# A feed-forward block whose weights are streamed in 128-column tiles and split beside the products

## The reference

```python
def _lora_linear(x, w, a, b):
    base = jnp.einsum('bsd,od->bso', x, w)
    low = jnp.einsum('bsr,or->bso', jnp.einsum('bsd,rd->bsr', x, a), b)
    return base + low * SCALING          # SCALING = 2, rank 16
h1 = _lora_linear(x, w1, lora_A1, lora_B1)     # 512 -> 1376
h3 = _lora_linear(x, w3, lora_A3, lora_B3)     # 512 -> 1376
g = jax.nn.silu(h1) * h3
return _lora_linear(g, w2, lora_A2, lora_B2)   # 1376 -> 512
```

## Time and profile before

| | us |
|---|---|
| median of 3 runs | 2617.37 (2616.24 to 2623.03) |
| the profiled execution: its time | 2618.33 |
| its span, first to last instruction | 2616.4 |
| TensorE busy (matmul) | 2486.5 (95%) |
| VectorE busy | 1558.7 (60%) |
| ScalarE busy | 1355.7 (52%) |
| GpSimd busy | 1059.2 (40%) |
| mean granted TensorE clock | 0.975 of full speed |

### The profile page before, as it was taken

The page is one execution under the profiler, slowest core; times in us unless marked ns, Lnnn a source line. Parts: engine busy times, 40 slices in busy tenths (PEclk is TensorE's granted clock), DMA queues, the critical chain, the costliest instruction groups (busy, mean ns, idle before and its releaser), DMA issues. The chain is left out here.

```text
span 2616.4 us, 40097 instructions
## 1 busy us (share of the span) xinstructions
PE 2486.5 (95%) x12487; PEld 1839.7 (70%) x12487; DVE 1558.7 (60%) x2791; ACT 1355.7 (52%) x2088; POOL 1059.2 (40%) x1097
## 2 busy tenths in 40 slices
PE   6999999999999999999998599989999999999996
PEld 3677776777777777777774366667887878778774
DVE  5666666666666666666663611066657557557566
ACT  3577777777777777777774300033324324334231
POOL 0455565555556555555653100034234234343220
PEclk8999999999999999999998699989999999999998
DMA  5222222222222222221221500021010010010001
GB/s 190 48 47 55 43 54 49 46 51 51 51 43 54 47 48 51 45 57 43 54 44 57 160 6 0 0 81 41 0 40 16 24 40 16 24 40 16 1 1 53
DMA packets 46694, 116.86 MB, mean 45 GB/s; under 512 B 5313, under 2 KB 22721, under 8 KB 40514
## 3 DMA queue, kind: packets, MB, share of 16 engines
q1 hardware_dynamic: 46658, 116.40, 17.0%
HBM read 71.81 MB, written 10.49 MB: 31 GB/s over the span
## 5 line engine op out<-in xcount | busy, mean ns | idle before, releaser
L472 DVE TENSOR_REDUCE row_max<-ps_max 128x1 f32<-128x512 f32 x1024 | 671.0, 688 | 198.5 <-PE ps_max L539 176.6
L390 POOL TENSOR_TENSOR p_lo<-probs,p_hi 128x1024 f16<-128x1024 f32 x256 | 547.8, 2150 | 387.4 <-ACT p_hi L422 387.1
L417 ACT ACTIVATE probs<-ps_score 128x1024 f32<-128x1024 f32 x512 | 523.2, 1022 | 253.3 <-PE ps_score L554 229.1
L552 PE MATMUL ps_score<-Q,K 128*128 128x512 f32 x1024 | 407.5, 398 | 1.6 <-ACT probs L417 1.5
L554 PE MATMUL ps_score<-Q,K 97*128 97x512 f32 x1024 | 407.0, 397 | 0.0
L539 PE MATMUL ps_max<-KX,Q 68*128 68x512 f32 x1024 | 378.6, 410 | 16.1 <-DMA KX<-content_k 10.3
L466 DVE TENSOR_TENSOR Q<-ps_x,Q 64x512 fp32r<-64x512 f32 x256 | 176.5, 689 | 247.2 <-ACT Q L412 243.5
L422 ACT ACTIVATE p_hi<-probs 128x1024 f16<-128x1024 f32 x256 | 269.5, 1053 | 4.1
L539 PEld LDWEIGHTS ps_max<-KX,Q 68*128 68x128 f32 x1024 | 188.7, 189 | 91.7 <-issue 40.2
L552 PEld LDWEIGHTS ps_score<-Q,K 128*128 128x128 f32 x1024 | 194.4, 190 | 60.9 <-ACT probs L417 13.4
L554 PEld LDWEIGHTS ps_score<-Q,K 97*128 97x128 f32 x1024 | 195.2, 191 | 38.8
(11 more groups left out here) (231 smaller groups left out, 4223.7 us busy)
## 6 DMA issues: line engine op xcount, KB each, us to landing
Q<-Q SPq DMA_DIRECT2D x64, 512.0 KB, 4.3
w_raw<-in_w_qrope SPq DMA_DIRECT2D x32, 512.0 KB, 3.7
wq_raw<-in_wq SPq DMA_DIRECT2D x8, 1024.0 KB, 5.5
wo_raw<-in_wo SPq DMA_DIRECT2D x8, 1024.0 KB, 4.9
w_raw<-in_w SPq DMA_DIRECT2D x6, 704.0 KB, 4.2
Q<-content_q SPq DMA_DIRECT2D x64, 64.0 KB
K<-content_k SPq DMA_DIRECT2D x64, 64.0 KB
wkv_raw<-in_wkv SPq DMA_DIRECT2D x8, 512.0 KB, 3.5
```

Of the source, the lines that this page charges most:

```text
L390: pool.tensor_tensor(p_lo[:, j, :, :], probs[:, j, 0:PAIRED, :], p_hi[:, j, :, :], ALU.subtract)\
L417: act.activation(probs[:, j, 2 * half:2 * half + 2, :], ps_score[half][:, :, :], ACT.Exp, scale=SCALE).then_inc(exped, 1)
L472: dve.tensor_reduce(row_max[:, t, j:j + 1], ps_max[t % 2][:, :], axis=AXX, op=ALU.max)\
L552: pe.matmul(ps_score[half][:, k, :], K1[:, b, t * P:(t + 1) * P], Q1[:, b, j, :], start=True, stop=False)
```

## The change

The feed-forward block is rewritten, with the stage ahead of it.

- The weights w1, w3 and w2 are laid out in memory as 11 tiles of 128 hidden columns, each 128 x 1536 (1024 of w1 and w3, 512 of w2, 768 KB). The loop has 22 steps, one for each half and tile, written out; each step loads its tile (so each tile is loaded twice) into a ring of three.
- The up projections aren't folded any more. Instead u = A x is made once for each half by 12 matmuls (`low_rank`, L1050), scaled by 2, and each projection gets one more matmul, B u (L1069).
- The down weights are still folded, tile by tile: one matmul (`delta_out`, L1042), one addition by VectorE (`fold`).
- w1 and w3 tiles are rounded by ScalarE (L889) and subtracted by GpSimd two steps ahead. w2 and g are split too: 12 rounded matmuls (L1081) stand where four float32 ones stood.
- The factors and the first three tiles are loaded in `merge_heads_stage`, behind wo and x; the factors are split there by ScalarE (after tile 4) and VectorE (after tiles 4, 5 and 6), and the first two weight tiles as well.

The diff, cut to its core:

```diff
+            swiglu_first_loads(sp, dram, ffn)
+        @block.gpsimd
+        def _(pool):
+            for s in range(AHEAD):
+                swiglu_w_low(pool, ffn, s)
+            pool.wait_ge(ffn["w_low"], AHEAD)
...
+                if t == ST:
+                    swiglu_lora_high(act, ffn)
+                if ST < t <= ST + AHEAD:
+                    swiglu_w_high(act, ffn, t - ST - 1)
+            act.wait_ge(ffn["w_high"], AHEAD)
...
+                for part in {ST: (0, 1), ST + 1: (2,), ST + 2: (3, 4)}.get(t, ()):
+                    swiglu_lora_low(dve, ffn, part)
...
+def swiglu_load(sp, dram, m, s):
+    sp.dma_start(m["raw"][:, s % RAW, :], dram["w_ffn"][STEPS[s][1], :, :]).then_inc(m["raw_in"][s % RAW], 16)
...
+def swiglu_lora_high(act, m):
+    act.wait_ge(m["lora_in"], 64)
+    act.activation(m["a_hi"][:, :, :], m["a_raw"][:, :, :], ACT.Copy).then_inc(m["lora_high"], 1)
+    act.activation(m["b2"][:, :], m["b2_raw"][:, :], ACT.Copy).then_inc(m["lora_high"], 1)
+    act.activation(m["a2"][:, :], m["a2_raw"][:, :], ACT.Copy).then_inc(m["lora_high"], 1)
+    for i in range(2):
+        act.activation(m["b"][:, i, :], m["b_raw"][:, i, :], ACT.Copy).then_inc(m["lora_high"], 1)
...
+def swiglu_lora_low(dve, m, part):
+    rows = [slice(32 * k, 32 * (k + 1)) for k in range(3)]
+    dve.wait_ge(m["lora_high"], part + 1)
+    if part == 0:
+        out, raw, high = (m[name][:, :, :] for name in ("a_lo", "a_raw", "a_hi"))
+    elif part == 1:
+        out, raw, high = m["b2"][rows[1], :], m["b2_raw"][rows[1], :], m["b2"][rows[1], :]
+    elif part == 2:
+        out, raw, high = m["a2"][rows[2], :], m["a2_raw"][rows[2], :], m["a2"][rows[2], :]
+    else:
+        i = part - 3
+        out, raw, high = m["b"][rows[1], i, :], m["b_raw"][rows[1], i, :], m["b"][rows[1], i, :]
+    dve.tensor_tensor(out, raw, high, ALU.subtract).then_inc(m["lora_low"], 1)
...
+def swiglu_w_high(act, m, s):
+    act.wait_ge(m["raw_in"][s % RAW], 16 * (s // RAW + 1))
+    act.activation(m["w_hi"][:, s % RING, :, :, :].rearrange("p i c n -> p (i c n)"), m["raw"][:, s % RAW, 0:W13],
+                   ACT.Copy).then_inc(m["w_high"], 1)
+def swiglu_w_low(pool, m, s):
+    pool.wait_ge(m["w_high"], s + 1)
+    pool.tensor_tensor(m["w_lo"][:, s % RING, :, :, :].rearrange("p i c n -> p (i c n)"), m["raw"][:, s % RAW, 0:W13],
+                       m["w_hi"][:, s % RING, :, :, :].rearrange("p i c n -> p (i c n)"), ALU.subtract)\
+        .then_inc(m["w_low"], 1)
+AHEAD = 2
...
+        ps_down, ps_h, ps_delta, ps_u = banks[0:4], banks[4:6], banks[6], banks[7]
...
+            for s in range(RAW, NS):
+                sp.wait_ge(w_low, s - RAW + 1)
+                sp.wait_ge(w2_low, s - RAW + 1)
+                swiglu_load(sp, dram, mem, s)
...
+            def second(s):
+                pool.wait_ge(w2_high, s + 1)
+                pool.tensor_tensor(w2_lo[:, s % RING, :], raw[:, s % RAW, W13:W13 + D], w2_hi[:, s % RING, :],
+                                   ALU.subtract).then_inc(w2_low, 1)
+            for s in range(NS):
+                second(s)
+                if s + AHEAD < NS:
+                    swiglu_w_low(pool, mem, s + AHEAD)
...
+            for s, (half, m) in enumerate(STEPS):
+                if m == 0:
+                    act.wait_ge(u_made, half + 1)
+                    act.activation(u[:, :], ps_u[0:SLOTS, :], ACT.Copy, scale=LORA_SCALE).then_inc(u_high, 1)
+                act.wait_ge(folded, s + 1)
+                if s >= RING:
+                    act.wait_ge(down, s - RING + 1)
+                act.activation(w2_hi[:, s % RING, :], raw[:, s % RAW, W13:W13 + D], ACT.Copy).then_inc(w2_high, 1)
+                if s + AHEAD < NS:
+                    if s + AHEAD >= RING:
+                        act.wait_ge(hidden[1], s + AHEAD - RING + 1)
+                    swiglu_w_high(act, mem, s + AHEAD)
+                act.wait_ge(hidden[0], s + 1)
+                if s:
+                    act.wait_ge(g_made, s)
+                act.activation(gate[:, :], ps_h[0][:, :], ACT.Silu).then_inc(gated, 1)
+                act.wait_ge(g_made, s + 1)
+                if s >= 2:
+                    act.wait_ge(down, s - 1)
+                act.activation(g_hi[:, s % 2, :], g[:, s % 2, :], ACT.Copy).then_inc(g_high, 1)
...
+            def fold(s):
+                dve.wait_ge(delta, s + 1)
                 dve.wait_ge(raw_in[s % RAW], 16 * (s // RAW + 1))
+                dve.scalar_tensor_tensor(out=raw[:, s % RAW, W13:W13 + D], in0=ps_delta[:, :], scalar=LORA_SCALE,
+                                         in1=raw[:, s % RAW, W13:W13 + D], op0=ALU.mult, op1=ALU.add).then_inc(folded, 1)
+            def low_u(half):
+                dve.wait_ge(u_high, half + 1)
+                dve.scalar_tensor_tensor(out=u[64:SLOTS, :], in0=ps_u[64:SLOTS, :], scalar=LORA_SCALE,
+                                         in1=u[64:SLOTS, :], op0=ALU.mult, op1=ALU.subtract).then_inc(u_low, 1)
+            def add_out(half):
+                dve.wait_ge(down, HT * (half + 1))
+                    row = X[:, half * ST + t, :]
+                    dve.tensor_tensor(row, ps_down[t][:, :], row, ALU.add).then_inc(taken, 1)
+            def count_out(half):
+                    dve.wait_ge(taken, half * ST + t + 1)
+                    dve.bn_stats(sb["stats"][:, half * ST + t, :], X[:, half * ST + t, :]).then_inc(counted, 1)
+            for s, (half, m) in enumerate(STEPS):
+                if s == 0:
+                    fold(0)
+                if m == 0:
+                    low_u(half)
+                if s + 1 < NS:
+                    fold(s + 1)
+                if half and m == 1:
+                    add_out(0)
+                dve.wait_ge(gated, s + 1)
+                dve.wait_ge(hidden[1], s + 1)
+                if s >= 2:
+                    dve.wait_ge(g_low, s - 1)
+                dve.tensor_tensor(g[:, s % 2, :], ps_h[1][:, :], gate[:, :], ALU.mult).then_inc(g_made, 1)
+                dve.wait_ge(g_high, s + 1)
+                dve.tensor_tensor(g_lo[:, s % 2, :], g[:, s % 2, :], g_hi[:, s % 2, :], ALU.subtract).then_inc(g_low, 1)
+                if half and m == 1:
+                    count_out(0)
+            add_out(1)
+            count_out(1)
...
+            TERMS = ((0, 0), (1, 0), (0, 1))
+            x = (xh, xl)
+            def delta_out(s):
+                m = STEPS[s][1]
+                if s:
+                    pe.wait_ge(folded, s)
+                pe.matmul(ps_delta[:, :], mem["a2"][:, m * P:(m + 1) * P], mem["b2"][:, :], start=True, stop=True)\
                   .then_inc(delta, 1)
+            def low_rank(half):
+                a = (mem["a_hi"], mem["a_lo"])
+                k = 0
+                for i, j in TERMS:
+                    for c in range(DC):
+                        last = pe.matmul(ps_u[0:SLOTS, :], a[i][:, c, :], x[j][:, c, half * S:(half + 1) * S],
+                                         start=k == 0, stop=k == 3 * DC - 1)
+                        k += 1
+                last.then_inc(u_made, 1)
+            def project(s, half, m):
+                pe.wait_ge(w_low, s + 1)
+                w = (w_hi, w_lo)
                 for i in range(2):
+                    if s:
+                        pe.wait_ge((gated, g_made)[i], s)
                     k = 0
+                    for part, j in TERMS:
                         for c in range(DC):
+                            pe.matmul(ps_h[i][:, :], w[part][:, s % RING, i, c, :], x[j][:, c, half * S:(half + 1) * S],
+                                      start=k == 0, stop=False)
                             k += 1
+                    if m == i == 0:
+                        pe.wait_ge(u_low, half + 1)
+                    pe.matmul(ps_h[i][:, :], mem["b"][:, i, m * P:(m + 1) * P], u[:, :], start=False, stop=True)\
+                      .then_inc(hidden[i], 1)
+            def project_down(s):
+                half, m = STEPS[s]
+                pe.wait_ge(g_low, s + 1)
+                pe.wait_ge(w2_low, s + 1)
+                if half and m == 0:
+                    pe.wait_ge(taken, ST)
+                gs, ws = (g_hi, g_lo), (w2_hi, w2_lo)
+                for t in range(ST):
+                    for k, (i, j) in enumerate(TERMS):
+                        last = pe.matmul(ps_down[t][:, :], gs[i][:, s % 2, t * P:(t + 1) * P], ws[j][:, s % RING, :],
+                                         start=m == k == 0, stop=m == HT - 1 and k == 2)
+                last.then_inc(down, 1)
+            delta_out(0)
+            for s, (half, m) in enumerate(STEPS):
+                if m == 0:
+                    low_rank(half)
+                if s + 1 < NS:
+                    delta_out(s + 1)
+                project(s, half, m)
+                if s:
+                    project_down(s - 1)
+            project_down(NS - 1)
```

More of the change, by code:

```diff
@@ L796 @@
 RAW = 3
-LR = 3 * 32
+RING = 3
+SLOTS = 3 * 32
+W13 = 2 * DC * P
```

(20 more changed lines are left out.)

202 lines of the change are left out of this document (49 added, 153 removed).

## The result

| | before | after |
|---|---|---|
| median us (lowest to highest) | 2616.8 (2613.1 to 2623.0) | 2579.74 (2576.49 to 2582.48) |
| ratio, 95% interval | | 0.9853 [0.9835, 0.9871] |
| the profiled execution, its span | 2618.33, 2616.4 | 2582.48, 2580.4 |
| mean granted clock | 0.975 | 0.983 |

What follows compares the result with a forecast made beforehand. TensorE, busy for 95% of the span, was taken as the bound. Starting at 1468.4 us, plus 202.0 for matmuls, 1.7 clock and 0.3 to the add gives 1672.4 against 1709.15: forecast 2581 us, range 2574 to 2592.

Steps and rivals of the forecast that it cites:

- stage ahead: Stage before the norm: early loads and splitting of factors and weight tiles lengthen it by 2.5 us (0 to 6).
- 882 matmuls: Feed-forward products over 22 steps: each matmul costs 0.229 us, together 202.0 us against 196.7 before.
- clock at the start: First feed-forward matmuls, after the pause behind the norm: lower clock level loses 1.7 us (0 to 2.2).
- behind it: Everything after the add of the last feed-forward outputs: claimed unchanged.
- The stretch: From the norm's end to the first projection: the whole wait goes, TensorE beginning at 1465.9 instead of 1511.15, 45.2 us.
- The loop: Feed-forward steps: TensorE alone sets the pace, 39 matmuls in 8.93 us; the loop itself gets 5.3 us longer.
- Rival A: Feed-forward loop: TensorE loses 0.1 us at each of six semaphore places per step, 13 us, giving 2594; chance 0.09.
- Rival C: Feed-forward loop: rounded matmuls take 0.215 us, half a full record, 12 us better, giving 2569; chance 0.03.
- Rival E: Whole change: something counted as hidden takes the gain's place one for one, within 0.3% of before; chance 0.02.
- the meeting: VectorE's factor subtractions beside GpSimd's weight subtractions before the norm: one waits for the other, making the lengthening 2.5, not 1.3 us.
- Rival B: Stage before the norm: the factors load late and stretch it by 5 to 10 us, giving 2586 to 2591; chance 0.06.
- Rival D: Feed-forward loop: weight stream becomes the bound if loads exceed some 13 us; at 18 us, 2636 us; chance 0.03.

Runs made afterwards that it cites:

- e3: Changed kernel without the 44 products of B and u, so the output lacks the low-rank part of h1 and h3: 2572.47 us, ratio 0.9816.
- e4: Changed kernel with GpSimd's subtractions of the first two weight tiles moved to the start of the feed-forward stage: 2579.22 us, measured once.
- e2: Changed kernel with four full-fp32 down products per step instead of twelve rounded ones, same work on the other engines: 2597.73 us, ratio 0.9912.
- e9: Changed kernel with the edit of e7, and w2's folded high and low parts kept for the second half: 2575.43 us, ratio 0.9841.
- e7: Changed kernel with the two last subtractions of the factors' low parts moved behind the first fold in the feed-forward stage: 2580.3 us, ratio 0.9862.
- e8: Changed kernel with five more loads of each weight tile into a spare buffer, ahead of each used load: 2650.13 us, ratio 1.0126.
- e6: Changed kernel with each weight tile load from the fourth on issued one step later: 2595.02 us, ratio 0.9908.
- e1: Changed kernel with the factors and first weight tiles loaded and split where the kernel before did it: 2589.63 us, ratio 0.9873.

## Why the prediction held, step by step

| step | forecast | measured |
|---|---|---|
| what lies ahead of all | unchanged | -0.8 (third turn, 1425.10 against 1425.88) |
| stage ahead | +2.5 (0 to 6) | +1.6 (29.92 against 28.28) |
| norm | unchanged | -0.2 (10.98 us against 11.19) |
| norm to first matmul | 0.55 | 0.51 |
| 882 matmuls | 202.0 | 202.6 (0.2297 each) |
| clock at the start | 1.7 (0 to 2.2) | 1.5 here; 0 in e3 and e4 |
| last matmul and seam | 0.3 | 0.4 |
| the add at | 1672.4 | 1671.01 |
| behind it | unchanged | +2.1 |
| span | 2579.6 | 2580.4 |

*The stretch.* Read from a busy share of 0.42 at half clock and a list of waits in which no entry was TensorE's own; it went whole. The sum of its 45.2 us came true because the three things that could have taken its place, loads, the stage ahead and the norm's end, had been timed one by one.

*The loop.* 0.229 us for each matmul, whatever it does, gives the step to 0.03 us, adding (e2: full products back, the block 15.1 us longer where 15.0 were forecast) and removing (e3: 8.47 us against 8.50; e9). Rival A (gaps at six semaphores) has 0.04 us in 204.5 for it. Rival C falls too: the 215.7 ns that the Trainium skill gives (TensorE: Matmul & The Clock Gate, "Wait — 56ns, not 53.3ns?") were not seen for rounded operands in any run here, 0.229 to 0.230 at the full clock in each. Rival E, the gain taken up one for one elsewhere, falls with the span's 36 us.

*The stage ahead* is the term that was mis-sized, 1.6 instead of 2.5 us. Without the meeting I had 1.3, and e4 measures 1.2 (29.48 against 28.28); the meeting was put at 1.2 us more and costs 0.44. VectorE's 2.4 us at the port are paid mostly out of waits for TensorE that it would have had, and what counts is the two subtractions ahead of the last add (e7: without them nothing is left of the 1.64 us). I had let everything behind the meeting slide without looking for the slack that takes it up. Rival B did not come: ScalarE begins on the factors at 1433.98 with no wait in its row, and TensorE's sixth tile is made at 1441.03, without a stall.

*Rival D* was given the right mechanism, and a threshold of 13 us where the corrected equation has 12.6 (an estimate; the runs bound it from below only, by 8.7 us without loss). e8 shows what it does when it decides, e6 that it needs only one step of issue time, and at three to six times the price that I worked out for that experiment.

*What came right by luck.* The add was 1.4 us earlier than forecast, and 2.1 us were lost behind it, which no step had; they cancel to 0.8. And "everything ahead is unchanged" could have been off by more than any term: the stage ahead begins (TensorE's first turn) between 1410.74 and 1418.01 us in the thirteen profiles, with the same code up to there; in the two that are compared it was 1414.25 and 1413.78.

## What to carry to other kernels

A stretch in which the bounding engine is half busy at half clock is worth nearly its whole length if the work in it can be expressed as a few more passes of that engine: here 22 deltas, 24 passes for u and 44 for `B u` (20.6 us) stand for 45 us of folding, and the weights come in finer pieces, so that the products start with the first tile. Which of the two counts for how much was not tried. For a ring, write the cycle out as an equation (steps x pace = load + the engines between request and release) and solve it for the pace; the queue that stands behind the request counts too. Before pricing a delay on an engine that isn't the bound, look for its next wait: that much of the delay is free.

## What the runs showed of the hardware that was not expected

- The granted clock fell to the lower level (0.50) for some 3 us, some 1.2 us after TensorE had taken up work behind a wait of 1.28 to 1.30 us: behind 6 of 91 such waits in thirteen profiles, 1.5 to 1.7 us lost each time.
- Behind the same pause of 2.13 us the feed-forward products start at the full level in some executions (e3, e4: 0.23 us each) and drop to the lower one for up to eight matmuls in others (after: 3.38 us for eight): 0 to 1.5 us. In e1, behind a pause of 6.32 us, the first dozen took 0.43 us each. Bounds from one profile are not enough for this term.
- 342 GB/s of loads beside it cost TensorE nothing (150 of 150 us busy).
